# Attention with top-k tokens and a linear layer on one core: a new order of V's parts, of selection, statistics and pv's exits, and of two banks

## The reference

```python
q, k, v = (split_heads(layernorm(x) @ W + b) for W, b in ...)   # 16 heads of 64
ctx = local_attention(q, k, v)        # block of 128 queries against 256 keys around it
idx = [0] + top_62_by_norm(q) + [1023]
ctx[idx] = softmax(q[idx] @ k.T / 8) @ v          # these 64 tokens see all keys
x = x + merge_heads(ctx)
```

## Time and profile before

| | us |
|---|---|
| median of 3 runs | 2053.85 |
| slowest of the 3 | 2055.9 |
| profiled execution, its own time | 2058.4 |
| its span from the first to the last instruction | 2056.8 |
| TensorE busy | 1995.7 |
| VectorE busy | 1518.9 |
| ScalarE busy | 1001.0 |
| GpSimd busy | 602.7 |

### The profile page before, as it was taken

One profiled execution on the slowest core, in us unless ns is written; L12 is line 12 of the kernel. 1 busy time (PEld: TensorE's weight loads), 2 busy tenths in 40 slices (PEclk: granted clock), 3 DMA queues, 4 the chain that ended last, 5 costly groups with the idle time before them and its releaser, 6 DMA issues.

```text
span 2056.8 us, 36785 instructions
## 1 busy us (share of the span) xinstructions
PE 1995.7 (97%) x11264; PEld 1664.1 (81%) x11264; DVE 1518.9 (74%) x2917; ACT 1001.0 (49%) x1435; POOL 602.7 (29%) x478
## 2 busy tenths in 40 slices
PE   6999999999999999999999999999999999999999
PEld 6877878788878787887787888887888878888887
DVE  5597888865978888659788886588777877666664
ACT  4326666673266667732576676326666761000000
POOL 2333233224332232243322322433233103221211
PEclk9999999999999999999999999999999999999999
DMA  3438766754386767643867665327777654333331
GB/s 123 144 104 170 151 155 148 137 117 141 104 168 149 150 155 129 122 144 95 173 148 155 153 128 117 108 80 153 151 166 166 129 119 176 137 127 141 134 122 72
DMA packets 533830, 280.79 MB, mean 137 GB/s; under 512 B 433264, under 2 KB 498870, under 8 KB 533680
## 3 DMA queue, kind: packets, MB, share of 16 engines
q1 hardware_dynamic: 505584, 186.76, 42.3%
q0 software_dynamic: 23776, 76.63, 12.3%
q10 hardware_dynamic: 4320, 15.73, 1.9%
HBM read 122.73 MB, written 51.44 MB: 85 GB/s over the span
## 4 chain that ended last, share of the span: by engine, by line
PE 79%; DVE 8%; issue 5%; DMA 4%; ACT 2%; POOL 1%; SPq 1%; DVEq 0%; ACTq 0%; POOLq 0%
PE proj L649 42%; PE proj L810 16%; PE pv L768 8%; PE pv L790 3%; PE score L756 2%; PE turn L756 2%; DVE p_parts L1521 2%; DMA p_turned<-p_parts 2%; DMA v_turned<-q_sq 1%; PE turn L799 1%; PE score L782 1%; PE turn L688 1%; PE proj L928 1%; ACT pT L1144 1%; DVE neg_max L1538 1%
## 5 line engine op out<-in xcount | busy, mean ns | idle before, releaser
L649 PE MATMUL proj<-xT_hi,w_lo 128*128 128x512 f32 x1536 | 420.7, 403 | 0.0
L649 PE MATMUL proj<-xT_hi,w_hi 128*128 128x512 f32 x1536 | 414.0, 413 | 5.7 <-POOL w_lo L458 3.2
L649 PE MATMUL proj<-xT_lo,w_hi 128*128 128x512 f32 x1536 | 383.3, 392 | 0.0
L456 POOL CAST w_hi<-w_raw 128x1024 fp32r<-128x1024 f32 x96 | 105.8, 1102 | 871.1 <-PE proj L649 673.8
L649 PEld LDWEIGHTS proj<-xT_lo,w_hi 128*128 128x128 f32 x1536 | 289.7, 189 | 64.2
L1144 ACT COPY pT<-p_turned 128x1024 uint16<-128x1024 uint16 x256 | 331.8, 1370 | 7.3 <-DMA p_turned<-p_parts 7.2
L649 PEld LDWEIGHTS proj<-xT_hi,w_lo 128*128 128x128 f32 x1536 | 285.4, 192 | 60.5
L649 PEld LDWEIGHTS proj<-xT_hi,w_hi 128*128 128x128 f32 x1536 | 282.1, 193 | 64.2 <-issue 6.3
L1521 DVE COPY p_parts<-probs 128x1024 uint16<-128x1024 uint16 x320 | 250.7, 805 | 74.9 <-DMA p_turned<-p_parts 21.7
L768 PEld LDWEIGHTS pv<-v_nat,pT 128*128 128x128 f32 x2048 | 253.2, 196 | 47.6 <-issue 37.1
L768 PE MATMUL pv<-v_nat,pT 128*128 128x65 f32 x2048 | 251.9, 277 | 30.0 <-DVE ctx_out L1557 17.2
(11 more groups left out here) (179 smaller groups left out, 3036.4 us busy)
## 6 DMA issues: line engine op xcount, KB each, us to landing
w_raw<-in_wstream POOLq DMA_DIRECT2D x94, 512.0 KB
x_buf<-in_rows SPq DMA_DIRECT2D x41, 512.0 KB, 3.8
q_rows<-pT SPq DMA_DIRECT2D x64, 256.0 KB
ctx_rows<-ctx_out SPq DMA_DIRECT2D x128, 128.0 KB, 2.4
out<-q_store ACTq DMA_DIRECT2D x30, 512.0 KB, 2.6
q_store<-in_cols POOLq DMA_DIRECT2D x28, 512.0 KB, 5.2
q_store<-ctx_rows SPq DMA_DIRECT2D x28, 512.0 KB, 4.1
x_buf<-in_rows POOLq DMA_DIRECT2D x14, 512.0 KB, 5.1
```

The lines of the kernel that those rows point to most:

```text
L456: pool.tensor_copy(w_hi[b][:, :], w_raw[b][:, :]).then_inc(w_hi_set, 1)
L649: mm = pe.matmul(proj[:, bank, :], w[b][:, k * P:k * P + P], x[:, k, half * HALF:half * HALF + HALF], start=(m == 0), stop=(m == 23), skip ...
```

## The change

Edits, engine by engine (with the numbers of units, not `hp`):

- TensorE: in unit 7, part 6 is issued before the global scores and the third weighing, as in all other units. The linear rows use the banks of `proj` the other way round.
- VectorE: the first piece of V of unit 1 is parted before the last three selection steps and not behind `top_rows`; the second and third pieces move up by one place each. In every unit `pv_out` of the second weighing comes before a selection step and the part of V, and in units 2 to 8 `pv_out` of the previous unit's fourth weighing comes before the third part of V. Stage 0 of the roots moves from unit 3 to unit 2, stage 1 within unit 3 to stage 0's place, and `turn_stats` from the end of unit 3 to stage 1's place.
- ScalarE: the second half of V's projection for unit 1 is taken out before `norms_out`. All three joins of V in unit 1 stand around the first exponentials. In unit 7 V's second half is taken out before the third join of P.
- SP: in unit 1 the third transpose of V is issued before the first ones of P.
- POOL: the split of V's slice for unit 2 comes before the store of the first selection.

```diff
             def stores(n, hp, following):
                 turn_p(n, hp, 0)
-                turn_v(n, hp, 2)
                 if hp > 0:
+                    turn_v(n, hp, 2)
                     store_ctx(n, hp - 1, STEPS - 1)
...
-                for k in range(2):
+                for k in range(V_PIECES):
                     turn_v(n, 0, k)
...
+                split_pair(n, "v", 1)
                 store_rows(n, 0)
-                split_pair(n, "v", 1)
...
-                    mm = pe.matmul(proj[:, half, :], x[b][:, k * P:k * P + P], w[:, k, half * 512:half * 512 + 512],
+                    mm = pe.matmul(proj[:, 1 - half, :], x[b][:, k * P:k * P + P], w[:, k, half * 512:half * 512 + 512],
...
-                        pe.wait_ge(proj_free[b], BATCH * BANK_USES[b] + 1)
+                        pe.wait_ge(proj_free[1 - b], BATCH * BANK_USES[1 - b] + 1)
...
-                if not early:
-                    part_of(n, hp, 6)
+                part_of(n, hp, 6)
                 global_scores(u)
                 weigh(u, 2)
-                if early:
-                    part_of(n, hp, 6)
...
+                if opens:
+                    join_v(n, hp, 0)
                 for h in range(2):
                     exps(u, 0, h)
+                if opens:
+                    for k in range(1, V_PIECES):
+                        join_v(n, hp, k)
...
-                join_p(n, hp, 2)
                 if early:
                     out("v", 1, 2)
+                join_p(n, hp, 2)
...
+                v_out(n, 0, 1)
                 norms_out(n, 1)
-                v_out(n, 0, 1)
...
-                    part_v(n, 0, 1)
+                    part_v(n, 0, 2)
...
-                part_v(n, hp, 2)
                 if hp > 0:
                     pv_out(u - 1, 3)
+                    part_v(n, hp, 2)
...
                 if following and hp == HALF_PAIRS - 2:
-                    row_roots(n, 0)
+                    row_roots(n, 1)
...
+                pv_out(u, 1)
                 top_norms(4)
                 if not last:
                     part_v(n, hp + 1, 1)
-                pv_out(u, 1)
+                if following and hp == HALF_PAIRS - 3:
+                    row_roots(n, 0)
                 if following and hp == HALF_PAIRS - 2:
-                    row_roots(n, 1)
+                    turn_stats(n)
...
+                        if r == 2 * HALF_PAIRS - 1:
+                            part_v(n, 0, 0)
                         for step in range(3 * r, 3 * r + 3):
                             top_find(n, 0, step)
...
                 top_rows(n, 0)
-                part_v(n, 0, 0)
+                part_v(n, 0, 1)
```

More of the change, by code:

```diff
@@ L827, in linear_ahead @@
                         pe.wait_ge(ahead_split, b + 1)
-                        pe.wait_ge(proj_free[b], BATCH * BANK_USES[b] + 1)
+                        pe.wait_ge(proj_free[1 - b], BATCH * BANK_USES[1 - b] + 1)
                     else:
                         pe.wait_ge(ahead_out[b], half)
-                mm = project(b, half, b, part, lo_ready)
+                mm = project(b, half, 1 - b, part, lo_ready)
                 if part == 1:
@@ L856, in attend @@
                 opens = isinstance(hp, int) and hp == 0
-                early = isinstance(hp, int) and hp == PAIRS - 2
                 scores(n, hp, 0)
@@ L1182, in attend @@
                 join_p(n, hp, 0)
-                join_v(n, hp, 0)
+                if not opens:
+                    join_v(n, hp, 0)
                 out("v", 0, 0)
@@ L1190, in attend @@
                 join_p(n, hp, 1)
-                for k in range(1, V_PIECES):
-                    join_v(n, hp, k)
+                if not opens:
+                    for k in range(1, V_PIECES):
+                        join_v(n, hp, k)
                 if last:
@@ L1602, in out_ahead @@
                 dve.wait_ge(ahead_done[b], half + 1)
-                dve.tensor_tensor(ahead_hb[b][:, cols], proj[:, b, :], ahead_hb[b][:, cols], ALU.add).then_inc(ahead_out[b], 1)
+                dve.tensor_tensor(ahead_hb[b][:, cols], proj[:, 1 - b, :], ahead_hb[b][:, cols], ALU.add).then_inc(ahead_out[b], 1)
             def lin_moments(t, b, turn2):
@@ L1721, in attend @@
                 pv_out(u, 2)
-                if following and hp == HALF_PAIRS - 2:
-                    turn_stats(n)
                 columns(4)
@@ L1814, in lin_out @@
                     dve.wait_ge(o_stored[b], 16 * turn2 + 16)
-                dve.tensor_tensor(lin_o[:, b, cols], proj[:, half, :], lin_hb[:, b, cols], ALU.add).then_inc(o_set, 1)
+                dve.tensor_tensor(lin_o[:, b, cols], proj[:, 1 - half, :], lin_hb[:, b, cols], ALU.add).then_inc(o_set, 1)
             with dve.Fori(0, REST // 2 - 1) as j:
```

## The result

The changed kernel took 2082.68 us (median of 4 executions: 2069.18, 2073.86, 2091.5 and 2091.68), the kernel before 2053.85 beside it. The ratio is 1.0135, with a 95% interval of 1.01 to 1.017: slower by 1.35%, where 2032.5 was predicted. Ten more executions, on another chip, gave 2057.65 to 2093.64 with a median of 2074.97. Two of them, 2089.2 and 2093.64, count as slow ones and are not in the ratio of 1.0089 (1.0053 to 1.0125). The kernel before lay between 2045 and 2065 in all its executions, the changed one between 2057 and 2092 without those two, so the change also made the time less certain. The profiled execution is the one of 2069.18.

A forecast was written before the change was run, and what follows sets the result against it. TensorE was taken as the bound, its waits and clock losses lengthening units beyond 37.11 us. Gains 26.7 + 12.0 - 0.6 + 0 - 16.8 = 21.3 us; 2058.4 - 21.3 - 4.55 = 2032.5 us, 8 times in 10 between 2009 and 2041.

The forecast's parts named there:

- Unit 4 and the exits: Unit 4, all passes: roots and statistics moved, pv's exits earlier on VectorE; gain 12.0 us, bounds 7.5 to 12.0.
- Unit 1: Unit 1, four passes: parting V earlier removes TensorE's waits on v_nat, w_lo, ctx_out and the clock's losses; gain 26.7 us.
- Unit 7: Units 7 and 8, three passes: 6.6 us each saved, 6.8 given back waiting for xT_hi; net 0.6 us lost.
- The rival that it keeps its gain: Unit 7 into 8: x^T's columns come 3 us earlier, so nothing is given back; 2012 us; chance 0.12.
- The linear banks: Linear rows, last pass: the wait on kT_lo is replaced by one on w_lo; gain 0, at best 0.8 plus 1.7.
- POOL's split moved: Unit 1's selection: POOL's split holds VectorE's small instructions, TensorE waits 2.5 us for qT_lo plus 1.7 of clock; costs 16.8 us.
- the rival: Unit 1's selection: small instructions aren't held by POOL's split; the wait costs 2.8 us, not 16.8; 2018.5 us; chance 0.25.
- a late transfer of V: Unit 1: V's last piece lands 4.2 us later, costing 26.4 us in all; 2059 us, 0.25% slower; chance 0.04.

The follow-up runs named there:

- `after_yield`: The changed kernel, with GpSimd's split at the end of units 1 to 7 waiting for VectorE's last two copies of P: 2052.31 us, ratio 0.9979 to the kernel before.
- the second profile: The changed kernel run again with nothing edited, on another chip: profiled execution 2059.05 us, median of all ten 2074.97 us.

## Why the prediction was wrong, point by point

- **What failed first: "Unit 4 and the exits" has a gain and no price.** Its "I cost them at nothing" is said of the moved stages of the roots alone; for what the earlier exits of pv do to the end of later units the sum has no term at all, and the runs put +28.1 us there in the first profile. The gain of 12.0 us in unit 4 is there to the tenth. What the step left out is who starts by TensorE's progress and not by VectorE's: GpSimd's split at the unit's end. TensorE's stall in unit 4 had let VectorE get ahead. Without it the copies at unit 5's end, whose margins were +0.13, +0.59 and +0.59 in passes 1 to 3, begin behind w_hi (with both exits moved, -0.37, -0.34 and -0.38). The one exit alone costs 1.17%, both cost 1.42%, and nothing with GpSimd's wait (0.9979).
- **What failed besides: the sizes, seen without collisions.** With GpSimd's wait the ratio is 0.9979, a gain of about 4 us and not 21.3, so the collisions gave the wrong sign and are not the whole miss. The profile of `after_yield`, 4.7 us shorter than that of the kernel before, goes: unit 1 -7.1 (forecast -26.7), unit 4 -9.5 (-12.0), unit 7 -19.1 (-19.8), unit 8 with what follows, qT_lo included, +22.1 (+37.2), and units 2, 3, 5 and 6 together +8.9 (0).
- **Unit 1: mechanism right, size wrong.** V's waits went and TensorE is busy for 33.93 us in pass 1, but of 26.7 us came 11.7 in the first profile and 3.1 in the second. The timeline of the changed kernel, unit 1 of pass 1:

```profile
154.54 3.35 DVE L1524 COPY p_parts<-probs 128x1024 uint16<-128x1024 uint16 x2 [0.36 <-DVE top_idx L1480]
165.29 1.11 PE L768 MATMUL pv<-v_nat,pT 128*128 128x65 f32 x8 [1.44 <-ACT pT L1140]
182.40 1.99 PE L768 MATMUL pv<-v_nat,pT 128*128 128x65 f32 x16 [1.99 <-DVE ctx_out L1560]
```

  P's parts, held by GpSimd's next split, are now what is late, and then pv's exit. I took the "clean length" of a unit as what remains when its named wait goes; that holds only if nothing else was within 3.4 us of it. I had also taken the short wait on ctx_out as gone (0.83 us before, at 182.67): it is 1.99 us, and in the second profile the clock fell behind it. The collisions at unit 1's end are the other part of that step's price.
- **Unit 7: right in both halves.** Unit 7 is 37.3, and xT_hi is awaited 3.23, 3.37 and 3.18 us (3.4 forecast). The rival that it keeps its gain fell. The net, forecast at 0.6 us lost, is 2.3 us gained in the first profile, and undoing the order cost 3.4 to 9.6 us, so the new order is better than forecast.
- **The linear banks: right.** The wait on kT_lo is gone, and TensorE waits 3.0 us at the same place (the row with issue as its end), so nothing was gained. The profile doesn't name what it waited for; w_lo of the linear rows ends at 1661.24 and TensorE begins at 1661.35, which fits the forecast wait on it.
- **POOL's split moved: right in kind, too dear.** The small instructions are held, against the rival:

```profile
142.87 2.46 DVE L1492 TENSOR_SCALAR idx_row<-idx_f,row_base 8x64 f32<-8x64 f32 x1
142.88 2.40 POOL L458 TENSOR_TENSOR w_lo<-w_raw,w_hi 128x1024 fp32r<-128x1024 f32 x1
149.45 0.50 PE L756 MATMUL score<-kT_hi,qT_hi 64*128 64x192 f32 x4 [1.82 <-DVE qT_lo L1456]
```

  0.23 us became 2.46, in passes 1 to 3. TensorE waited 1.8 us and not 2.5, at clock 1.00 afterwards, and only 0.29 in pass 4, where the split begins behind the small instructions and idx_row takes 0.23: 5.9 us of the 16.8. The clock was luck: in the second profile the same wait of 1.87 us in pass 1 was followed by a granted clock of 0.53 (149.65 to 152.00). The Trainium skill's rule that the later one waits for the whole instruction (SBUF — State Buffer, Who interferes with whom) agrees with the length of this row, on 8 partitions: idx_row ends at 145.33 and w_lo at 145.28. Which of the two came first the row doesn't tell, as they begin 0.01 us apart.
- **The rivals.** The only one on the slow side, a late transfer of V, didn't happen. Collision of copies with the split was in my own argument for one place, and I didn't ask it of the ends of the units.

What stays open: what makes the margins differ between executions of one kernel (at unit 1's end they mostly go with the granted clock; at unit 5's end no run shows a reason), how a collision's price parts between the hold and the late transposes, and how the executions near 2091 look inside. The roots' stage 0 was not told apart from VectorE's general lack of slack.

## What to carry to other kernels

When a wait of the bounding engine is removed, look at what starts by that engine's progress and shares a resource with the next-slowest engine; list the margin between the two at every stage end, and treat one of a few tenths of a microsecond as a loss to come (here +0.13 and +0.59 were used up). If two engines hold each other up there, order them by a semaphore: GpSimd's wait for the copies took some 22 us off the changed kernel. It is no free insurance, for it cost the kernel before 0.31%. A table of margins against durations, over all stages of one profile, shows before any run which margins are thin; in the kernel before it has the first step (copies of 2.27 us and not 1.43), but what a negative margin costs only the changed kernels showed. And a gain that holds in one profile may hang on the clock granted behind a wait: read a second execution before it is booked.

## What was not expected of the hardware

The hold is a cliff. At the ends of units 1 to 6, with a margin of 0.6 us or more the pair of copies took 1.43 us (but for five of up to 2.20), with +0.04 to +0.59 it took 2.27 to 2.31 (the second copy ends behind w_hi), and with -0.02 to -0.38 it took 4.16 to 4.51 (the first copy ends behind w_hi, the second behind w_lo). Later still the pair gets shorter again, as less of the split is left to hold it: 3.82 at -0.71, 3.41 at -1.40, 3.05 at -1.77. The step from +0.6 to just below zero thus costs VectorE about 3 us, and TensorE 4 to 7 by the end of the next unit (units 2, 3 and 6 behind such a pair were 41.2 to 44.5 us and not 37.1).
